# One exponential over both heads of a key step in the full attentions of a decoder kernel

## The reference

```python
scores = jnp.einsum('bhqd,bhkd->bhqk', Q, K) / jnp.sqrt(jnp.float32(D_K))   # D_K = 8, 16 heads
scores = jnp.where(keep, scores, NEG)          # causal, a mask, or a key bias; nothing in layer 2
attn = jax.nn.softmax(scores, axis=-1)
x = jnp.einsum('bhqk,bhkd->bhqd', attn, V)
```

## Time and profile before

| | |
|---|---|
| median of 3 runs | 5208.85 us |
| the profiled execution's own time | 5211.14 us |
| its span, first to last instruction | 5209.3 us |
| instructions in the trace | 126790 |
| granted TensorE clock, mean of the span | 0.881 |

### The profile page before, as it was taken

One profiled execution on the slowest core, in us unless ns is written; L12 is line 12 of the kernel. 1 busy time (PEld: TensorE's weight loads), 2 busy tenths in 40 slices (PEclk: granted clock), 3 DMA queues, 4 the chain that ended last, 5 costly groups with the idle time before them and its releaser, 6 DMA issues. The chain is left out here.

```text
span 5209.3 us, 126790 instructions
## 1 busy us (share of the span) xinstructions
PE 4082.8 (78%) x45549; PEld 2393.4 (46%) x45678; DVE 3267.1 (63%) x5972; ACT 2659.0 (51%) x5482; POOL 1243.4 (24%) x2886
## 2 busy tenths in 40 slices
PE   2005767876669897696996588999999999999997
PEld 1003333432332222343442236777777777777775
DVE  7995444544437676434555426777777777777775
ACT  2035723544547676451221345666666666666664
POOL 0011200111101111110000144444444444444443
PEclk6557977987779899797997678999999999999998
DMA  2000020000000000002440001000000000000000
GB/s 56 0 0 1 2 73 18 1 1 1 4 30 1 1 2 1 11 1 77 139 138 28 5 1 50 6 10 24 6 27 6 6 28 6 10 24 6 28 6 11
DMA packets 60831, 110.20 MB, mean 21 GB/s; under 512 B 11399, under 2 KB 43251, under 8 KB 59164
## 3 DMA queue, kind: packets, MB, share of 16 engines
q1 hardware_dynamic: 59558, 101.70, 6.7%
q0 software_dynamic: 784, 1.80, 0.2%
HBM read 96.06 MB, written 1.74 MB: 19 GB/s over the span
## 5 line engine op out<-in xcount | busy, mean ns | idle before, releaser
L676 DVE TENSOR_REDUCE minus_max<-banks 128x1 f32<-128x512 f32 (+4 forms) x1152 | 606.3, 570 | 320.1 <-PE banks L571 313.8
L641 ACT ACTIVATE probs<-banks 128x512 f32<-128x512 f32 (+4 forms) x1152 | 581.1, 556 | 337.9 <-PE banks L609 335.4
L2862 POOL TENSOR_TENSOR loc_cos_part<-loc_cos_part,loc_sin_part 128x512 f32<-128x512 f32 x388 | 494.4, 1274 | 672.0 <-DVE loc_sin_part L3291 671.4
L2935 PE MATMUL banks<-loc_w_qkv,loc_shifted 128*128 128x256 f32 x1552 | 391.7, 396 | 15.3 <-DMA loc_adder_of<-loc_head_ones 14.8
L609 PE MATMUL banks<-q_stack,k_stack 64*128 64x512 bf16 (+3 forms) x1152 | 254.1, 381 | 98.5 <-DMA q_stack<-max_rows 70.8
L3324 DVE TENSOR_TENSOR loc_headsT<-banks,loc_sum_inv 128x512 f32<-128x512 f32 x192 | 132.7, 691 | 291.7 <-ACT loc_sum_inv L3196 291.7
L2935 PEld LDWEIGHTS banks<-loc_w_qkv,loc_shifted 128*128 128x128 f32 x1552 | 282.1, 192 | 55.2 <-DMA loc_w_qkv<-in_L_ffn_Wqkv_dram 15.2
L622 PE MATMUL banks<-probs,pair_rows 128*32 128x512 f32 (+3 forms) x2304 | 295.6, 589 | 0.0
L3316 DVE TENSOR_REDUCE loc_minus_max<-banks 128x4 f32<-128x384 f32 x386 | 197.1, 552 | 152.1 <-PE banks L3002 151.3
L700 POOL CAST max_parts<-minus_max 128x8 bf16<-128x8 f32 x192 | 36.3, 189 | 1042.2 <-DVE minus_max L676 1042.2
L1888 PE MATMUL banks<-identity,srt_b 128*128 128x128 f32 x64 | 11.2, 320 | 344.6 <-DVE srt_b L2168 344.6
(11 more groups left out here) (520 smaller groups left out, 9408.0 us busy)
## 6 DMA issues: line engine op xcount, KB each, us to landing
expert_share<-limited_rows SPq DMA_DIRECT2D x136, 256.0 KB, 3.9
expert_w<-in_L_ffn_pairs_dram SPq DMA_DIRECT2D x84, 192.0 KB, 2.3
loc_w_qkv<-in_L_ffn_Wqkv_dram SPq DMA_DIRECT2D x7, 1536.0 KB, 7.8
expert_share<-grouped_rows SPq DMA_DIRECT2D x32, 256.0 KB, 4.1
q_stack<-max_rows SPq DMA_DIRECT2D x384, 3.0 KB
loc_v_edge<-loc_v SPq DMA_DIRECT2D x192, 32.0 KB, 1.7
fixed_w<-in_L_ffn_experts_dram SPq DMA_DIRECT2D x8, 514.5 KB, 3.6
loc_pack<-in_L_ffn_pack_dram SPq DMA_DIRECT2D x6, 537.5 KB, 4.0
```

Source lines behind the costliest of these rows:

```text
L641: nc.scalar.activation(probs[(a % 2) * C + k][e][0:kn, q0:S], t_bank[e][0:kn, q0:S], ACT.Exp, scale=scale).then_inc(s["exp_done"], 1)
L676: nc.vector.tensor_reduce(minus_max[:, u, e, qs[0]:qs[0] + len(qs)], view, AX.X, ALU.max, negate=True).then_inc(s["max_done"], 1)
L2862: nc.gpsimd.tensor_tensor(cos_part[:, tiles, :], cos_part[:, tiles, :], sin_part[:, tiles, :], ALU.add).then_inc(s["summed"], 1)
L2935: ins = nc.tensor.matmul(g.bank[3 * j][:, (t % 2) * QK:(t % 2 + 1) * QK], xs[:, t * P:(t + 1) * P], w_qkv[:, ds(at, QK)], start=True, stop ...
```

## The change

`act_exp` issues one exponential for a key step where it issued two. The two probability buffers of a step become one buffer of twice the width, whose halves the values' matmuls read as before; the exponential reads banks 5 and 6 as one operand of (keys, 2, queries); it waits for both turned matmuls, and when it ends it raises `exp_done` by 2. The waits on TensorE stay as they are written, so that the one of head 0 is now fulfilled at the same moment as the one of head 1.

```diff
-        probs = [[sbuf(f"probs{i}_{e}", [P, S]) for e in range(2)] for i in range(2 * C)]
+        both = [sbuf(f"probs{i}", [P, 2, S]) for i in range(2 * C)]
+        probs = [[pair[:, e, :] for e in range(2)] for pair in both]
...
+        t_banks = g.banks[:, 5:7, :]
...
         def act_exp(act, n, b, a, k):
             k0, kn = ktiles[k]
             q0 = k0 if causal else 0
-            for e in range(2):
-                act.wait_ge(s["turned_ready"], n * 2 * C + (2 * k + e + 1))
-                act.wait_ge(s["values_done"], quads_of(b, a) * C + (k + 1))
-                nc.scalar.activation(probs[(a % 2) * C + k][e][0:kn, q0:S], t_bank[e][0:kn, q0:S], ACT.Exp,
-                                     scale=scale).then_inc(s["exp_done"], 1)
+            act.wait_ge(s["turned_ready"], n * 2 * C + (2 * k + 2))
+            act.wait_ge(s["values_done"], quads_of(b, a) * C + (k + 1))
+            nc.scalar.activation(both[(a % 2) * C + k][0:kn, :, q0:S], t_banks[0:kn, :, q0:S], ACT.Exp,
+                                 scale=scale).then_inc(s["exp_done"], 2)
```

## The result

The changed kernel takes 5240.71 us (median of 5 runs, 5234.43 to 5243.18); the kernel before, beside it, 5209.04 (5 runs). The ratio is **1.0053, interval 1.0041 to 1.0064**: slower by 0.5%, where no change was forecast and the range ended at 5219. The profiled execution took 5241.27 us, its span 5239.5. Of the nine executions of the kernel before that ran beside experiments 6 and 7, one took 10738.33 us at a granted clock of 0.405; it is in their median (5211.67), but not in their ratios.

A forecast was written before the change was run, and what follows sets the result against it. Neither TensorE nor ScalarE is full, so the chain through both was taken as the bound. Terms of -0.6 (differential), -1.0 (causal) and +0.8 (masked) sum to -0.8 us: 5208.0 us against 5208.85, no change, range 5200 to 5219.

The forecast's parts named there:

- the saving of 0.065 per pair: On ScalarE, one exponential over 1024 columns was to take 1.02 us, 0.06 to 0.07 less than the pair.
- which steps are short: Differential quad: even slot's k = 3, odd slot's k = 0 and 1, where TensorE waits tightly for exponentials; 1.49 to 1.57 us each.
- `max_rows` starts late: In a differential quad, `max_rows`, queued on ScalarE after k = 1, was to start 0.16 to 0.30 us late.
- the cover: In a differential quad, TensorE's existing wait for GpSimd's pieces of the maxima was to absorb ScalarE's 0.6 to 0.8 us lateness.
- The 0.02 us gained per quad: Differential calls: matmuls ahead of GpSimd's maxima come 0.02 us earlier in each of 32 quads, -0.6 us in all.
- Pieces, from rows 5: Handovers in a differential quad's short steps: exponential's end to matmul 0.05 us, second matmul's start to exponential 0.42 to 0.51.
- rival 1: Slower, short steps become the bound at the odd slot's k = 2 matmuls: about 5227 us, or 5219 to 5231; chance 0.12.
- The later steps find their exponentials long done: Differential quad, steps after GpSimd's wait: matmuls for values and stacks lie between, so TensorE needn't wait for exponentials.
- The pattern of one quad: One differential quad's timeline was applied to all 32 quads of the two differential calls, -0.02 us each.
- Masked call: Masked context call: head 0's mask matmul loses its head start, +0.05 us in 16 quads, +0.8 us; bounds 0 to +3.2.
- Causal call: Causal call: three steps per quad each 0.02 us shorter, -1.0 us in all; bounds -2.9 to +1.0.
- Context: Context calls of layers 0 and 1: next slot's matmuls wait for the DMA, so 0 change; bound -2.2 us.

The follow-up runs named there:

- experiments 6 and 7: 6: experiment 1 with the turned matmuls' wait set apart before each exponential, 5236.21 us; 7: changed kernel with TensorE's DMA wait taken early as its own instruction, 5241.34 us.
- experiment 2: The kernel before, still with two exponentials per step, but each raises `exp_done` by 2 and every wait for it is doubled; 5223.55 us.
- experiment 1: The changed kernel, but its one exponential raises `exp_done` by 1 and every wait for it is halved; 5224.78 us.
- experiment 4: As experiment 1, but the last three slots of every call use two exponentials again, with a separate semaphore for head 0; 5217.72 us.

## Why the prediction was wrong

- **Right:** the price of the exponential (1.02 forecast, 1.023 measured), the saving of 0.065 per pair, no cost for two banks, and which steps are short. `max_rows` starts late, as said, but by 0.66 us and not 0.16 to 0.30, counted from the exponential of k = 2 of the even slot. With the raise by 1 the short steps fit into the cover as forecast, by less than forecast: the steady quads measure 14.87 against 14.91, 14.87 against 14.87, 15.21 against 15.15. The 0.02 us gained per quad isn't seen.
- **The step that failed** is "Pieces, from rows 5: release to matmul 0.05 ... second matmul's start to its exponential 0.42 to 0.51". The size of both was carried over from the kernel before, though the change alters which instruction carries each wait. They were 0.05 to 0.15 and 0.49 to 0.64. The forecast gave the chain 0.12 to 0.26 us to spare at the odd slot's k = 2. From the exponential at 1658.87 to that matmul at 1664.94 are 6.07 us, where the kernel before has 5.80 and the forecast's pieces add up to 5.54 to 5.68: 0.4 to 0.5 more than forecast, and 0.27 more than before. The sum itself was also too kind: it names 0.50 as the upper bound of the handover and goes on with 0.45 twice; with 0.50 each time 0.02 us are left to spare, and not 0.12. This is rival 1, "when the handover takes longer than 0.5", which had a chance of 0.12; its place was right (1664.93, L611 after L642), its cause was not named. The raise by 2, read in the diff, was costed at nothing without naming a cover. Experiments 2 and 6 put it at 12 and 11 us, of which the lower clock in single quads is a part (4.5 us in the profile of experiment 2); the 16 us between experiment 1 and the changed kernel hold the later first matmul of a slot as well. The tail, below, is 7 us, and 5 of the 29 stay open.
- **"The later steps find their exponentials long done"** rested on the steps with other work of TensorE between. From the odd slot's k = 3 to the even slot's k = 0 it was a near thing: 1658.53 to 1660.06 is 1.53 us, and 0.51 + 1.02 + 0.14 = 1.67 is what the changed kernel takes.
- **"The pattern of one quad"** stood for 16. The last three quads of a call have no cover: 0.2, 0.8 and 0.9 us there in experiment 1. Experiment 4 put pairs back there and was 7 us shorter; the last two quads of the six calls are 5.3 us shorter together in its profile. A timeline of the call's end would have shown it.
- **Masked call:** +0.05 per quad forecast, at most 0.2; measured -0.04 to +0.2 with the raise by 1, most often 0.07 to 0.14. The working was right in kind. That the cover at GpSimd's wait didn't hold all of it is likely, but not shown.
- **Causal call:** -1.0 forecast; with the raise by 1 most steady quads are 0.03 to 0.13 shorter, so the sign was right, and in the changed kernel it is +5.5. **Context:** 0 forecast; -3.2 to +0.4 by the two pairs of profiles, where two profiles of the changed kernel differ by up to 2.9.
- The sentence of the Trainium skill (Perfetto Trace Analysis, Optimizing Scalar/DVE Operations), by which breaking up instructions lets work end sooner where an engine isn't saturated but holds others up, holds here only where nothing covers the wait: pairs in the last three slots gave back 7 us (experiment 4), while the steady quads are as long with one exponential as with two (14.87 against 14.91). The rival that it stood for was given too little.

What stays open: the last 5 us between experiment 4 and the kernel before; what decides which of two waits stands on a weight load; and why the granted clock falls at those quads and not at others. The section on the change says that the waits on TensorE stay as they are written. Their text does; in most slots, which instruction carries them at the first matmul doesn't (24 slots against 12 before).

## What to carry to other kernels

When two instructions become one, look at how the one waits and signals, not only at what it computes: a semaphore raised by 2 took the wait off the instruction, and 0.02 to 0.05 us at each handover, with 0.09 more at a slot's first matmul, undid on a chain without slack what the merge saved. Count the semaphore in the new unit, so that it rises by 1, and look in the new trace for which instruction carries the last wait. And read the end of a loop as well as its middle, since the work that covers a delay is often work for later iterations.

## What the runs showed of the hardware

- An exponential that raises its semaphore by 2 carries no wait: 576 wait instructions stand ahead, with a median of 278 ns, against 306 that pass in 17 ns when it raises by 1. In the odd slots it then starts 0.49 to 0.51 us after its matmul where 0.45 to 0.46 is had, and 0.54 with the wait set apart by hand. In the even slots, where the wait stands on a register instruction in both, it is 0.55 to 0.59 against 0.53 to 0.54 (medians by step over the steady quads of the first differential call).
- A matmul whose weight load carries the wait starts 0.06 us after the exponential's end; one whose wait stands in an instruction ahead of it, 0.14 to 0.15.
- An activation that reads two neighbouring banks, 128x1024, takes 1023 ns: 167 + 1024 x 0.836, with nothing for the second bank.
- Stretches at 1.2 GHz instead of 2.4 come in three of the changed kernel's quads at the same place in two executions (15.84, 16.95, 12.32 us), and each costs 1.3 to 2.2 us; the one in the causal call (16.56) doesn't.
